# A float32 graph layer on one core: column groups of 7, 1, 6 and 2 blocks in place of 6, 2, 6 and 2

## What is computed

```python
N, D_IN, D_OUT = (8192, 128, 128)
h = jnp.maximum(_layernorm(x, axis=-1), 0.0)
support = jnp.matmul(h, W)
out = jnp.matmul(adj, support) + b
x = x + jax.nn.relu(out)
```

## Time and profile before

| | us |
|---|---|
| median of 3 runs (721.60 to 721.69) | 721.62 |
| the profiled execution | 721.9 |
| its span in the profile | 720.1 |
| PE busy | 715.2 |
| DVE busy | 623.3 |
| ACT busy | 517.5 |
| moved by DMA | 281.60 MB, 391 GB/s over the span |

### The profile page before, as it was taken

One profiled execution on the slowest core, in us unless ns is written; L12 is line 12 of the kernel. 1 busy time (PEld: TensorE's weight loads), 2 busy tenths in 40 slices (PEclk: granted clock), 3 DMA queues, 4 the chain that ended last, 5 costly groups with the idle time before them and its releaser, 6 DMA issues.

```text
span 720.1 us, 7905 instructions
## 1 busy us (share of the span) xinstructions
PE 715.2 (99%) x3113; PEld 583.8 (81%) x3113; DVE 623.3 (87%) x394; ACT 517.5 (72%) x400; POOL 181.4 (25%) x99
## 2 busy tenths in 40 slices
PE   9999999999999999999999999999999999999998
PEld 4878888888888888888888888888888888888886
DVE  5999999999999888988798888878788887888895
ACT  2788888888888767766577667667676676767662
POOL 4445555556544402410041000000000000033023
PEclk9999999999999999999999999999999999999999
DMA  9999999999999999999999999999999999999992
GB/s 353 408 408 409 409 411 415 412 415 416 417 415 414 418 421 407 415 387 404 359 410 428 383 402 396 364 397 386 379 390 391 382 391 385 398 403 397 389 382 77
DMA packets 45110, 281.60 MB, mean 391 GB/s; under 512 B 5137, under 2 KB 5777, under 8 KB 31505
## 3 DMA queue, kind: packets, MB, share of 16 engines
q1 hardware_dynamic: 44496, 280.25, 97.2%
q10 hardware_dynamic: 576, 0.85, 0.4%
HBM read 276.89 MB, written 4.19 MB: 390 GB/s over the span
## 4 chain that ended last, share of the span: by engine, by line
PE 94%; DMA 3%; DVE 1%; SPq 0%; ACT 0%; issue 0%; DVEq 0%; ACTq 0%
PE banks L585 93%; DMA raw<-adj 3%; DVE low L543 1%; PE banks L612 0%; PE banks L613 0%; PE banks L611 0%; SPq L270 0%; ACT high L404 0%; DVE h_low L489 0%; DVE x_sb L505 0%; DVE x_sb L513 0%; SPq L267 0%; DVEq L175 0%; SPq L285 0%; ACTq L403 0%
## 5 line engine op out<-in xcount | busy, mean ns | idle before, releaser
L543 DVE TENSOR_TENSOR low<-raw,high 128x3072 fp32r<-128x3072 f32 (+3 forms) x261 | 576.5, 2235 | 83.1 <-PE banks L585 69.9
L404 ACT ACTIVATE high<-raw 128x3072 fp32r<-128x3072 f32 (+3 forms) x261 | 483.6, 1864 | 188.6 <-DMA raw<-adj 160.7
L585 PE MATMUL banks<-high,h_high 128*128 128x512 f32 x1012 | 272.7, 390 | 0.1
L585 PE MATMUL banks<-high,h_low 128*128 128x512 f32 x1012 | 272.0, 389 | 0.0
L585 PE MATMUL banks<-low,h_high 128*128 128x512 f32 x1012 | 268.5, 389 | 0.0
L585 PEld LDWEIGHTS banks<-high,h_high 128*128 128x128 f32 x1012 | 189.6, 188 | 41.1 <-ACT high L404 1.6
L585 PEld LDWEIGHTS banks<-low,h_high 128*128 128x128 f32 x1012 | 189.7, 188 | 40.1 <-DVE low L543 0.8
L585 PEld LDWEIGHTS banks<-high,h_low 128*128 128x128 f32 x1012 | 190.0, 188 | 39.5
L356 POOL TENSOR_SCALAR x_sb<-x_sb,bias 128x512 f32<-128x512 f32 x16 | 54.5, 3409 | 414.2 <-DMA x_sb<-x_blocks 414.2
L347 POOL TENSOR_SCALAR z_sb<-x_sb,neg_mean,rstd 128x128 f32<-128x128 f32 x60 | 94.7, 1590 | 1.6
L332 POOL TENSOR_TENSOR rstd<-var_eps,minus_half 128x4 f32<-128x4 f32 (+2 forms) x17 | 31.6, 1860 | 112.8 <-DVE var_eps L447 103.6
(11 more groups left out here) (34 smaller groups left out, 47.8 us busy)
## 6 DMA issues: line engine op xcount, KB each, us to landing
raw<-adj SPq DMA_DIRECT2D x106, 1536.0 KB, 8.6
raw<-adj SPq DMA_DIRECT2D x82, 768.0 KB, 10.6
raw<-adj SPq DMA_DIRECT2D x69, 512.0 KB, 11.9
x_sb<-x_blocks SPq DMA_DIRECT2D x16, 256.0 KB, 8.4
out_blocks<-x_sb SPq DMA_DIRECT2D x15, 256.0 KB, 8.7
x_sb<-x SPq DMA_DIRECT2D x14, 256.0 KB, 12.2
raw<-adj SPq DMA_DIRECT2D x3, 256.0 KB, 6.5
raw<-adj ACTq DMA_DIRECT2D x1, 256.0 KB, 2.8
```

The costliest lines, as they stand in the source:

```text
L404: nc.scalar.activation(high[:, t % HIGH_SLOTS, cols], raw[:, t % RAW_SLOTS, cols], ACT.Copy).then_inc(high_ready, 1)
L543: nc.vector.tensor_tensor(low[:, t % LOW_SLOTS, cols], raw[:, t % RAW_SLOTS, cols], high[:, t % HIGH_SLOTS, cols].bitcast(F32), ALU.subtra ...
L585: return nc.tensor.matmul(banks[:, FIRST_BANK[g] + c, :], h[:, (t - FIRST_STEP[g]) * DEPTHS[g] + k, :], tile[:, slot, at:at + BANK], start ...
```

## The change

- The groups are 7, 1, 6 and 2 blocks wide and 1, 6, 1 and 3 tiles deep. A step of the first group is now 7 pairs (1.84 MB, 21 matmuls), of all others 6. There are 64 + 11 + 64 + 22 = 161 steps.
- Three raw slots of 7 pairs stand in place of four of 6; the load of step t now waits for the low part of step t - 3.
- Only step 0 is done in four passes: 7 pairs, before 12.
- Pieces: step 0 [1,1,2,3]; the first group [3,2,2] up to step 19, then [4,3]; the third group [3,3], before whole.
- `statistics(3)`, the sums of tiles 8 to 11, moves behind the low parts of step 2; their rectifying moves from step 5 to step 6. The early halves of h now cover tile 1 too, and come ahead of `statistics(2)`.
- The residual x has six slots (two in z_sb) and is loaded two steps ahead of its drain step, behind the store on SyncE. Drain steps have a list for each group; finish comes 3 and store 8 steps after the drain, before 4 and 9.
- TensorE's wait for free banks where a group opens is made part by part.

```diff
-WIDTHS = [6, 2, 6, 2]
-DEPTHS = [1, 3, 1, 3]
-FIRST_BLOCK = [0, 6, 8, 14]
-FIRST_BANK = [0, 6, 0, 6]
+WIDTHS = [7, 1, 6, 2]
+DEPTHS = [1, 6, 1, 3]
+FIRST_BLOCK = [0, 7, 8, 14]
+FIRST_BANK = [0, 7, 0, 6]
...
-RAW_SLOTS, HIGH_SLOTS, LOW_SLOTS = 4, 3, 2
+RAW_SLOTS, HIGH_SLOTS, LOW_SLOTS = 3, 3, 2
...
-FOUR_PASS = 2
-
-NARROW_UNTIL = 24
+FOUR_PASS = 1
+
+NARROW_UNTIL = 20
...
+RES_SLOTS = 6
...
-DRAIN_AT = [3, 6, 8, 11, 13, 16]
-PROJECT_AFTER, FINISH_AFTER, STORE_AFTER = 1, 4, 9
+
+DRAIN_AT = [[1, 2, 4, 5, 7, 8, 15], [8], [3, 6, 8, 11, 13, 16]]
+RESIDUAL_AHEAD, PROJECT_AFTER, FINISH_AFTER, STORE_AFTER = 2, 1, 3, 8
...
     g = group_of(t)
     if t == 0:
-        return [1, 1, 2, 2]
+        return [1, 1, 2, 3]
     if g == 0:
-        return [3, 3] if t < FOUR_PASS or t >= NARROW_UNTIL else [2, 2, 2]
+        return [4, 3] if t < FOUR_PASS or t >= NARROW_UNTIL else [3, 2, 2]
+    if g == 2:
+        return [3, 3]
     return [1] * WIDTHS[g] if t == LAST else [WIDTHS[g]]
...
-    if t in (2, 5):
+    if t in (2, 6):
         return 2 if t == 2 else 3
...
-            if FIRST_STEP[g + 1] + DRAIN_AT[c] + after == t:
+            if FIRST_STEP[g + 1] + DRAIN_AT[g][c] + after == t:
                 return FIRST_BLOCK[g] + c
...
+
+        def residual(n):
+
+            slot = n % RES_SLOTS
+            return x_sb[:, slot, :] if slot < X_SLOTS else z_sb[:, slot - X_SLOTS, :]
...
@@ -274,13 +283,16 @@
                 if n < X_SLOTS:
 
                     sp.wait_ge(z_ready, TILES - EARLY)
+                elif n < RES_SLOTS:
+
+                    sp.wait_ge(h_low_ready, TILES - EARLY)
                 else:
-                    sp.wait_ge(stored[n % X_SLOTS], 16 * (n // X_SLOTS))
-                sp.dma_start(x_sb[:, n % X_SLOTS, :], x_blocks[n]).then_inc(res_landed[n % X_SLOTS], 16)
+                    sp.wait_ge(stored[n % RES_SLOTS], 16 * (n // RES_SLOTS))
+                sp.dma_start(residual(n), x_blocks[n]).then_inc(res_landed[n % RES_SLOTS], 16)
 
             def store(n):
                 sp.wait_ge(output_ready, n + 1)
-                sp.dma_start(out_blocks[n], x_sb[:, n % X_SLOTS, :]).then_inc(stored[n % X_SLOTS], 16)
+                sp.dma_start(out_blocks[n], residual(n)).then_inc(stored[n % RES_SLOTS], 16)
...
-                n = drained_at(t, 0)
-                if n is not None:
-                    load_residual(n)
                 n = drained_at(t, STORE_AFTER)
                 if n is not None:
                     store(n)
+                n = drained_at(t, -RESIDUAL_AHEAD)
+                if n is not None:
+                    load_residual(n)
...
-            whole(1)
-            statistics(2)
             for t in range(FOUR_PASS, EARLY):
                 early_halves(t)
-            statistics(3)
+            statistics(2)
             for t in range(FOUR_PASS, ALL_STEPS):
                 if t >= LOW_SLOTS + FOUR_PASS:
...
@@ -545,6 +555,8 @@
                                             ALU.subtract).then_inc(low_ready, 1)
                     if part == (0 if t >= NARROW_UNTIL else len(parts_of(t)) - 1) and rectified_at(t) is not None:
                         rectified_low(rectified_at(t))
+                if t == 2:
+                    statistics(3)
                 if mean_at(t) is not None:
                     mean(mean_at(t))
...
-                if opens and g >= 2:
-
-                    pe.wait_ge(output_ready, FIRST_BLOCK[g - 1])
 
                 def with_high(part):
                     pe.wait_ge(high_ready, halved(t, part))
+                    if opens and g >= 2:
+
+                        pe.wait_ge(output_ready, FIRST_BANK[g] + parts[part][1][-1] + 1)
                     if part == 0:
                         high_is_there(t)
                     for k in depths:
```

More of the change, by code:

```diff
@@ L214, in gnn_layer @@
         x_first_landed = sem("x_first_landed")
-        res_landed = [sem(f"res_landed{s}") for s in range(X_SLOTS)]
+        res_landed = [sem(f"res_landed{s}") for s in range(RES_SLOTS)]
         params_landed = sem("params_landed")
@@ L248, in gnn_layer @@
         output_ready = sem("output_ready")
-        stored = [sem(f"stored{s}") for s in range(X_SLOTS)]
+        stored = [sem(f"stored{s}") for s in range(RES_SLOTS)]
         block = ctx.enter_context(nc.Block())
+        def residual(n):
+            slot = n % RES_SLOTS
+            return x_sb[:, slot, :] if slot < X_SLOTS else z_sb[:, slot - X_SLOTS, :]
         def columns(t):
@@ L320, in _ @@
             sp.wait_ge(output_ready, n + 1)
-            sp.dma_start(out_blocks[n][:, 0:HALF], x_sb[:, n % X_SLOTS, 0:HALF]).then_inc(stored[n % X_SLOTS], 16)
-            for s in range(X_SLOTS):
-                sp.wait_ge(stored[s], 16 * (COL_BLOCKS // X_SLOTS + (s == n % X_SLOTS)))
+            sp.dma_start(out_blocks[n][:, 0:HALF], residual(n)[:, 0:HALF]).then_inc(stored[n % RES_SLOTS], 16)
+            for s in range(RES_SLOTS):
+                sp.wait_ge(stored[s], 16 * (len(range(s, COL_BLOCKS, RES_SLOTS)) + (s == n % RES_SLOTS)))
         @block.gpsimd
@@ L353, in _ @@
             for n in range(COL_BLOCKS):
-                pool.wait_ge(res_landed[n % X_SLOTS], 16 * (n // X_SLOTS + 1))
-                nc.gpsimd.tensor_scalar(x_sb[:, n % X_SLOTS, :], x_sb[:, n % X_SLOTS, :], bias[:, 0:1], None,
+                pool.wait_ge(res_landed[n % RES_SLOTS], 16 * (n // RES_SLOTS + 1))
+                nc.gpsimd.tensor_scalar(residual(n), residual(n), bias[:, 0:1], None,
                                         ALU.add).then_inc(x_biased, 1)
@@ L425, in _ @@
             act.wait_ge(output_ready, n + 2)
-            act.dma_start(out_blocks[n][:, HALF:BANK], x_sb[:, n % X_SLOTS, HALF:BANK]) \
-               .then_inc(stored[n % X_SLOTS], 16)
+            act.dma_start(out_blocks[n][:, HALF:BANK], residual(n)[:, HALF:BANK]) \
+               .then_inc(stored[n % RES_SLOTS], 16)
         @block.vector
@@ L504, in finish @@
                 dve.wait_ge(projected, n + 1)
[L505 to L506 removed]
+                nc.vector.scalar_tensor_tensor(residual(n), banks[:, bank_of(n), :], neg_bias[:, 0:1],
+                                               residual(n), ALU.max, ALU.add) \
                   .then_inc(output_ready, 1)
@@ L512, in finish_last @@
                 dve.wait_ge(last_projected, half + 1)
-                nc.vector.scalar_tensor_tensor(x_sb[:, n % X_SLOTS, cols], banks[:, half, 0:HALF],
-                                               neg_bias[:, 0:1], x_sb[:, n % X_SLOTS, cols],
+                nc.vector.scalar_tensor_tensor(residual(n)[:, cols], banks[:, half, 0:HALF],
+                                               neg_bias[:, 0:1], residual(n)[:, cols],
                                                ALU.max, ALU.add).then_inc(output_ready, 1)
```

2 lines of the change are left out of this document (removed).

## The result

| | before | after |
|---|---|---|
| median of 5 runs, us | 721.64 (721.60 to 722.16) | 742.16 (740.21 to 743.77) |
| profiled execution | 721.9 | 741.1 |
| its span | 720.1 | 739.3 |
| PE busy | 715.2 | 722.9 |
| DVE busy | 623.3 | 630.8 |

The change makes the kernel slower by 20.5 us: a ratio of 1.0281, 95% interval 1.0263 to 1.030. I had predicted 726.1 with a range of 722.4 to 730.5. The direction was right; the size was off by 16 us and the time lies outside the range. TensorE's granted clock is full in both, so none of it is the clock.

A forecast was written before the change was run, and what follows sets the result against it. TensorE was taken to bound the kernel, with 94% of the chain. The profiled 721.9 plus 2.2 for the start and 2.3 for the fourth group gave 726.4, a median of 726.1 us; range 722.4 to 730.5.

The forecast's parts named there:

- The start: Up to pair 42: low parts and sums crowd VectorE, TensorE stalls, pair 42 ends 2.2 us later.
- the bound of 3.3: At the start: slow GpSimd z of tiles 4 to 7 delays h_low, raising the loss from 2.2 to 3.3 us.
- The first group, the drains and the residual loads: First group and drain steps: same rate as before, VectorE 4.8 us level with TensorE in the fullest; no loss.
- The second group: 11 whole steps: three loops lag 4.2 us, covered by six projections and the low parts' head start; no stall.
- the lead: Whole steps: a low part is ready 3.1 us before TensorE wants it, behind the step's 12 high matmuls.
- L = 7.4: Whole-step loads, three slots: 7.4 us from issue to start of the high part; shortest row 7.0, median 8.6.
- the loop of the slots: Whole steps: load, high part and low part on one slot take 13.6 us, 1.4 over the 12.25 of three steps.
- The third group: 64 steps loaded in halves: the slot's loop takes about 11 us, so no stall.
- The fourth group: 22 whole steps: seven loops lag 9.5 us, less projections 4.1 and head start 3.1: stall 2.3 us.
- Rival 2: Fourth group: single transfers run late whatever the queue, loads 8 to 8.5 us, loss 6 to 10, 730 to 734; chance 0.13.
- The estimate from the skill: Whole-step loads: about 2.0 us plus bytes at 436 GB/s, 5.6 us, so the three-slot term would be 0.
- The two that I gave as tests: Fourth group: loads issued ever later, VectorE released by ScalarE; TensorE waiting for `low` in the last 60 us.

The follow-up runs named there:

- all_halves: The changed kernel with each step of the second and fourth groups loaded and cut in halves: 723.32 us, ratio 1.0021.
- before_3slots_halves: The kernel before the change with three raw slots and every step after the first group in halves: 723.31 us, ratio 1.0024.
- before_3slots: The kernel before the change with three raw slots in place of four, nothing else changed: 808.3 us, ratio 1.1195.
- old_groups_sums_later: The changed kernel with the old groups, four slots, one four-pass step, and the sums of tiles 8 to 11 behind step 3: 722.91 us, ratio 1.0020.

## Why the prediction was right or wrong

**The start: right in kind, 0.2 to 0.9 too large.** TensorE's first split matmul came at 12.80 (predicted 12.7), step 1 stalled 0.66 (0.4), step 2 0.26 (0.3), step 3 1.24 (1.8), and pair 43 started at 38.78, +2.0 where I said +2.2 with bounds of 1.4 to 3.3. By medians the start is worth 1.3 (723.32 against 722.04), since the kernel before does not run without a gap from 36.79 on, as I had read the earlier trace rows: step 7 takes 0.4 us more than its matmuls. The sums do stand between the low parts of steps 2 and 3, and TensorE waits for just that. VectorE's timeline of the kernel after:

```profile
17.90 4.03 DVE L553 TENSOR_TENSOR low<-raw,high 128x1536 fp32r<-128x1536 f32 x3 [1.03 <-ACT high L416]
21.85 0.68 DVE L501 SCALAR_TENSOR_TENSOR h_low<-z_sb,h_high 128x512 fp32r<-128x512 f32 x1
22.45 0.86 DVE L470 BATCH_NORM_STATS2 stats<-x_sb 128x6 f32<-128x128 f32 x4
```

and TensorE's, where the low matmuls of step 3 wait:

```profile
23.93 0.84 PE L597 MATMUL banks<-high,h_low 128*128 128x512 f32 x3
25.72 0.96 PE L597 MATMUL banks<-low,h_high 128*128 128x512 f32 x3 [0.95 <-DVE low L553]
```

The low parts of step 2 took 4.03 where I had 4.25, h_low 0.68 for 0.77, and TensorE came to step 3 at 23.25 where I had 22.8, which made the stall shorter. GpSimd's z of tiles 4 to 7 took 5.33 us from 11.70, between the 1.74 and the 10.13 of the earlier trace rows, and VectorE did not wait for h, so the bound of 3.3 did not come into play.

**The first group, the drains and the residual loads: right.** The rest of the first group is level. In all_halves, which has every drain, residual load and finish of the change, nothing stalls after pair 42. That level is 4.8 us of VectorE against 4.77 of TensorE was a fair reading. It holds only while the loads keep up: at 659 and 711 us of after the cut of a sum and a finish stand on the chain between two low parts.

**The second group: wrong.** I wrote 4.2 us of lag against six projections and the lead, no stall, and it stalled 2.7 us and another 1.4 behind it. The step that failed is L = 7.4 in the loop of the slots: the loads on the chain took 8.6 to 8.9. With 8.8 the loop is 8.8 + 2.78 + 3.36 + 0.1 = 15.0, and three of them lag 8.4 us, not 4.2. Against 4.1 of projections and 3.1 of lead that is a stall of 1.2 already; the eleven steps are nearer to three and a half loops than to three, and 1.4 us more make 2.6.

**The third group: right.** Its halves close the loop, though more barely than my 11 us: before_3slots_halves has 11.8. What it stalls, it stalls in its first four steps, which start late behind the second group; in all_halves it is -0.2.

**The fourth group: the mechanism right, the term mis-sized, and that is most of the error, 11.5 of 16 us.** I named the loop, wrote it as L + 2.78 + 3.36 + 0.1, and took L = 7.4. It measured 8.6, issue to start of the high part, in the mean of the seven loads on the chain (8.5, and 0.1 from there to ScalarE). By my own formula that is 7 x (14.86 - 12.25) - 4.1 - 3.1 = 11.1, and 13.8 was measured, with the last steps in it. So L is the step that failed: 8.8 of the 11.5 us that this term was short come from it alone. Of the other 2.7, two parts can be placed. From 616.63 to the end of the last whole low part, 729.94, the chain takes 113.3 us, and TensorE's work for these 23 steps and six projections is 98.0: a lag of 15.3 where the formula, with seven loops, has 14.2. And the lead was not 3.1 at the end. The last two steps are taken block by block, so TensorE wants the low part of step 159 after six high matmuls, not twelve, 1.36 us earlier:

```profile
729.98 0.96 PE L597 MATMUL banks<-low,h_high 128*128 128x512 f32 x3 [1.25 <-DVE low L553]
```

That is 2.5 together. A slip of mine is small beside it: seven loops of 13.64 less 12.25 are 9.7 and not 9.5, so the term should have been 2.5.

Why was L wrong? Two rows bore on it. One was the shortest load of the trace, 7.0, one was the median, 8.6. I took a value near the first because the queue would be short. It was not empty: SyncE issues a load when one step has been cut, and the load of the step before it is then still under way, by 3.7 us in the mean of the fourth group. And each slot needs its own load: a late one is not made up for where the loop is longer than its time already. The median with three slots came out at the old one. From the page of after, to be held against the earlier trace rows:

```profile
raw<-adj SPq DMA_DIRECT2D x192, 768.0 KB, 8.0
raw<-adj SPq DMA_DIRECT2D x31, 1536.0 KB, 8.5
```

With 8.6 from the earlier trace rows the loop is 14.84, and the formula gives 10.9 for the fourth group and 0.6 for the second; with the start, 735.3. That is still 6.9 us short, but on the right scale. Rival 2 had this size of L (8 to 8.5), and I gave it 0.13 and let the range cut its upper part. Its reason, that single transfers run late whatever the queue, is shown only in part: a late one of the 16 completions is there, but so is the load ahead. It too was low, with 730 to 734, and counted only the fourth group.

**The estimate from the skill.** The Trainium skill, DMA: Bandwidth & Descriptors, "Anatomy of one DMA — SWDGE (gpsimd) path", would by its figures put a step's load at 5.6 us, an estimate by which there would be no loss in whole steps. That section is on single transfers that GpSimd issues, and the loads here are SyncE's, each with another ahead of it. No load of a whole step on the chain of after took under 7.6, and the shortest shown of before_3slots is 6.18. The measurement decides, and it does not test the figure for a load alone.

**Signs.** The two that I gave as tests (loads issued later step by step, VectorE released by ScalarE and TensorE waiting for `low` in the last 60 us) both came. The third, that waits in the second group mean a loop too short by over 1 us, came too: it was too short by 1.2 in the fourth group and 1.4 in the second. At the start, pair 43 was to begin at 39.0 and did at 38.78; the wait for `low` of 1.5 to 3 us came as one of 0.95, in a stall of 1.24.

## What to carry to other kernels

Before taking away a buffer, write down the loop of one slot (issue to use, plus each engine that must be done before the next issue) and hold it against slots times the step's time, with the median load of the trace and not its shortest: with one slot less the load ahead is still under way. Where it doesn't close, cut the load and the work on it into halves before paying for another slot: here halves with three slots took 808 to 723 us and 742 to 723, and halving the transfer without the work took back 2.6 of 15.2 us. Look also at what else the issuing engine waits for between two loads; a wait that four slots hide can show with three. A term that repeats turns 1 us of error in one latency into 7 over seven loops, so the range belongs there.

## What the hardware showed that I had not expected

- A load of 1.5 MB took no less time with one slot less. With four slots its median from issue to landing was 8.6 us at a DMA share of 0.98 and 390 GB/s; with three, 8.5 in after and in before_3slots, at shares of 0.88 to 0.92 and 325 to 354 GB/s. In both the load ahead was still under way at the issue. Single ones on the chain took up to 9.99, and that one waited 2.9 us for the last of its 16 completions. Why one comes late is not shown.
- GpSimd's rstd of 128 x 4 took 1.01 us in the kernel before, and 7.65 at the same place in old_groups_sums_later (the first row is of before, the second of that kernel):

```profile
44.86 1.01 POOL L332 TENSOR_TENSOR rstd<-var_eps,minus_half 128x4 f32<-128x4 f32 x1 [19.09 <-DVE var_eps L447]
```

```profile
45.55 7.65 POOL L342 TENSOR_TENSOR rstd<-var_eps,minus_half 128x4 f32<-128x4 f32 x1 [8.28 <-DVE var_eps L457]
```

VectorE's timeline of that kernel has low parts without a pause beside the longer one:

```profile
45.37 6.97 DVE L551 TENSOR_TENSOR low<-raw,high 128x1024 fp32r<-128x1024 f32 x7
```

It ends at 53.20, 0.9 us after the last of them. In the kernel before, rstd had begun 0.12 us ahead of them (44.86 against 44.98). This goes further than the earlier trace rows: one small operation lasted through seven of VectorE's. The Trainium skill, SBUF — State Buffer, "Who interferes with whom", has GpSimd and a VectorE instruction with two SBUF inputs exclude each other, and this row agrees. No run here took it by itself.
